# Moving an output projection into the block of the attention loop, with its first units among the last attention steps

## The reference

```
x  : (8, 1024, 256)
xn = layernorm(x)
q, k, v = xn Wq' + bq, xn Wk' + bk, xn Wv' + bv      16 heads of 64
out = softmax(q k' / 8) v                              per batch and head
attn = out Wo' + bo                                    Wo: 256 x 1024
moe  = routed experts (64, top 8, at most 128 tokens each) + shared expert
y = x + attn(xn) + moe(xn)
```

## Time and profile before

| | |
|---|---|
| runs | 3563.14, 3563.44, 3565.11 us |
| profiled execution: its own time | 3562.05 us |
| its span, first to last instruction | 3560.3 us |
| mean granted TensorE clock | 0.992 of 2.4 GHz |
| PE busy | 3494.3 us, 98% |
| POOL, DVE, ACT busy | 2708.6, 2494.6, 1679.5 us |

### The profile page before, as it was taken

How to read it: one execution, slowest core, us unless ns; L and a number is a source line. 1 busy time by engine, 2 the same in 40 slices (tenths; PEclk the granted TensorE clock), 3 DMA queues, 4 the chain that set the end, 5 groups by cost and what they waited for, 6 DMA issues and landing times. The chain is left out here.

```text
span 3560.3 us, 60153 instructions
## 1 busy us (share of the span) xinstructions
PE 3494.3 (98%) x16416; PEld 2101.2 (59%) x16416; DVE 2494.6 (70%) x3255; ACT 1679.5 (47%) x3122; POOL 2708.6 (76%) x2339
## 2 busy tenths in 40 slices
PE   7999799999999999999999999999999999999899
PEld 6888555555555555555555555555555555555487
DVE  7888577777777777777777777777777777777344
ACT  4555344444444444444444444444444444444343
POOL 2111288888888888888888889888888888889521
PEclk9999899999999999999999999999999999999899
DMA  8777856666666666666666666666666666664396
GB/s 248 234 223 223 222 129 153 165 166 170 171 166 169 169 168 169 167 170 172 175 175 175 175 175 172 168 168 167 166 170 169 169 168 169 167 167 119 124 322 226
DMA packets 393678, 635.57 MB, mean 179 GB/s; under 512 B 48097, under 2 KB 214689, under 8 KB 393633
## 3 DMA queue, kind: packets, MB, share of 16 engines
q1 hardware_dynamic: 370848, 603.54, 61.2%
q0 software_dynamic: 14336, 23.08, 3.1%
q10 hardware_dynamic: 8448, 8.39, 0.7%
HBM read 306.91 MB, written 126.12 MB: 122 GB/s over the span
## 5 line engine op out<-in xcount | busy, mean ns | idle before, releaser
L1132 DVE TENSOR_REDUCE merged<-psum 128x1 f32<-128x1024 f32 x1024 | 1206.1, 1220 | 725.7 <-PE psum L857 724.9
L1093 ACT ACTIVATE probs<-psum 128x512 f32<-128x512 f32 x2048 | 1083.4, 600 | 1157.8 <-PE psum L831 826.6
L1314 POOL TENSOR_TENSOR sums<-sums,probs 128x512 f32<-128x512 f32 x768 | 980.0, 1276 | 96.5 <-ACT probs L1093 40.9
L1315 POOL TENSOR_TENSOR sums<-sums,probs 128x512 f32<-128x512 f32 x768 | 981.4, 1278 | 0.0
L872 PE MATMUL psum<-probs,v_sb 128*64 128x512 f32 x4096 | 931.9, 597 | 0.0
L828 PE MATMUL psum<-q_full,k_full 128*128 128x512 f32 x2048 | 877.1, 428 | 0.9 <-DVE low L1142 0.9
L831 PE MATMUL psum<-q_rest,k_rest 65*128 65x512 f32 x2048 | 811.9, 396 | 1.8 <-DMA q_rest<-minus_max 1.8
L872 PEld LDWEIGHTS psum<-probs,v_sb 128*64 128x64 f32 x4096 | 284.2, 137 | 561.0 <-issue 498.3
L828 PEld LDWEIGHTS psum<-q_full,k_full 128*128 128x128 f32 x2048 | 387.9, 189 | 197.1 <-issue 94.3
L1164 DVE RECIPROCAL sum_all<-sum_all 128x128 f32<-128x128 f32 x512 | 448.9, 919 | 28.3 <-ACT sum_all L1101 28.3
L831 PEld LDWEIGHTS psum<-q_rest,k_rest 65*128 65x128 f32 x2048 | 389.6, 190 | 63.5 <-DMA q_rest<-minus_max 2.1
(11 more groups left out here) (153 smaller groups left out, 3049.1 us busy)
## 6 DMA issues: line engine op xcount, KB each, us to landing
x_t<-xt SPq DMA_DIRECT2D x118, 1024.0 KB
k_full<-high SPq DMA_DIRECT2D x256, 256.0 KB
v<-values SPq DMA_DIRECT2D x64, 512.0 KB, 3.4
w_qk<-wqk_parts SPq DMA_DIRECT2D x64, 512.0 KB, 4.1
v_sb<-v SPq DMA_DIRECT2D x64, 512.0 KB, 4.7
q_full<-high SPq DMA_DIRECT2D x128, 256.0 KB
q_full<-low SPq DMA_DIRECT2D x128, 256.0 KB
k_rest<-low SPq DMA_DIRECT2D x128, 256.0 KB
```

Source lines behind the costliest of these rows:

```text
L1093: nc.scalar.activation(probs[:, kt, h, :], ring[ring_place(g, j) % RING], ACT.Exp, scale=SCALE).then_inc(probs_ready, 1)
L1132: nc.vector.tensor_reduce(out=merged[:, col:col + 1], in_=work[:, 2 * h:2 * h + 2, :].rearrange("p b c -> p (b c)"), axis=AX, op=ALU.max, ...
L1314: nc.gpsimd.tensor_tensor(sums[:, half, 0, :], first[:, 0, :], probs[:, kt, 0, :], ALU.add)
L1315: nc.gpsimd.tensor_tensor(sums[:, half, 1, :], first[:, 1, :], probs[:, kt, 1, :], ALU.add).then_inc(sums_added, 1)
```

## The change

The output stage is no block of its own any more; its instruction lists stand behind attention's in the same block. It gets its memory from attention's tiles: Wo's parts lie over `x_t`, `wo32` over `w_qk`, the loaded `ot` (`ot32_0`, `ot32_1`) over `high` and `low`, the high parts over `q_full` and `k_full`, the low parts over `q_rest` and `k_rest`, and x, `moe`, `rest` and y over `probs`. Therefore x and `moe` can only be loaded when attention's last P times V and last additions are done.

Work is put among the last steps:

- SP: `wo32`, `bv`, `bo` are loaded at the start of step 62 (`wo32` was loaded at the start of attention), unit 0's `ot` at the start of step 63, unit 1's after that. Behind the last store of attention come x and `moe` of unit 0, a wait for them, x and `moe` of unit 1, and then the loop over units 2 to 15.
- ACT: the weights' high part in four pieces in groups 2 and 3 of step 62 (`split_weights`), unit 0's high part in eight pieces in groups 1 and 2 of step 63 (`split_piece`), unit 1's at its end.
- DVE: the weights' low part in group 0 of step 63, the low parts of units 0 and 1 at its end, with the constant between.
- PE: at the end of step 63 both products of unit 0 with the constant's 32 small ones between, and then step 64 with the last `add_up` and P times V.

```diff
+    with ExitStack() as over:
+        ot32 = [over.enter_context(nc.sbuf_tensor(f"ot32_{par}", [P, PAIRS, HALF], F32)) for par in range(2)]
     high = sb("high", [P, 2, 2, N], F32R)
     low = sb("low", [P, 2, 2, N], F32R)
...
@@ tensor, end of step @@
+            if is_step(s, NP - 1):
+                pe.wait_ge(quad_reduced, QUADS * NP)
+                pe.wait_ge(wo_high, PIECES)
+                pe.wait_ge(wo_low, 1)
+                project(0, 0, 0)
+                pe.wait_ge(loaded_b, 2 * DMA)
+                for c in range(KD):
+                    for h in range(PAIRS):
+                        last = nc.tensor.matmul(psum[:, 7, c:c + 1], wo32[:, h, c * P:(c + 1) * P], bv[:, h:h + 1],
+                                                start=(h == 0), stop=(h == PAIRS - 1))
+                last.then_inc(const_filled, 1)
+                pe.wait_ge(y_weighted, NP)
+                project(0, 0, 1)
...
+        def output():
+            pe.wait_ge(const_ready, 1)
+            project(1, 1, 0)
+            project(1, 1, 1)
+            turn(0, 0)
+            project(2, 0, 0)
+            project(2, 0, 1)
+            turn(1, 1)
...
@@ scalar, step @@
+                    if is_step(s, NP - 2) and g >= 2 and n % 4 == 3:
+                        split_weights(2 * (g - 2) + n // 4)
+                    if is_step(s, NP - 1) and g >= 1 and n % 2 and 4 * g + n // 2 < 12:
+                        split_piece(4 * g + n // 2 - 4)
...
+            if is_step(s, NP - 1):
+                split_high(1, 1)
@@ vector, step @@
+                if is_step(s, NP - 1) and g == 0:
+                    dve.wait_ge(wo_high, PIECES)
+                    nc.vector.tensor_tensor(wo[:, LOW], wo32[:], f32(wo[:, HIGH]), ALU.subtract).then_inc(wo_low, 1)
+            if is_step(s, NP - 1):
+                split_low(0, 0)
+                dve.wait_ge(const_filled, 1)
+                dve.wait_ge(loaded_b, 2 * DMA)
+                nc.vector.tensor_tensor(const[:], psum[:, 7, 0:KD], bo[:], ALU.add).then_inc(const_ready, 1)
+                split_low(1, 1)
@@ sync, step @@
+            if is_step(s, NP - 2):
+                sp.wait_ge(lows_ready, 4 * NP)
+                sp.dma_start(wo32[:], io["wo"].rearrange("(h p) d -> p h d", p=P)).then_inc(loaded_w, DMA)
+                sp.dma_start(bv[:], io["bv"]).then_inc(loaded_b, DMA)
+                sp.dma_start(bo[:], io["bo"]).then_inc(loaded_b, DMA)
+            if is_step(s, NP - 1):
+                for half in range(2):
+                    sp.wait_ge(out_stored[half], DMA * PAIRS)
+                sp.wait_ge(placed, DMA * SHUFFLES * NP)
+                sp.wait_ge(quad_filled, QUADS * NP)
+                load_output(0, 0, 0)
...
             if att:
                 shift_out(s, par, 1)
+            if is_step(s, NP - 1):
+                for n in range(2):
+                    sp.wait_ge(ot_loaded[n], DMA)
+                load_output(0, 1, 1)
...
+        def output():
+            sp.wait_ge(pv_done, 4 * NP)
+            sp.wait_ge(sums_added, 14 * NP)
+            sp.wait_ge(scattered, DMA * NP)
+            load_rest(0, 0)
+            sp.wait_ge(xm_loaded, 2 * DMA)
+            load_rest(1, 1)
+            for half in range(2):
+                sp.wait_ge(out_stored[half], DMA * NP)
+            with sp.Fori(1, UNITS // 2) as i:
+                for par in range(2):
+                    u = i * 2 + par
+                    alone(sp, (loaded_w, DMA), (ot_loaded[0], DMA * u), (ot_loaded[1], DMA * u),
+                          (xm_loaded, 2 * DMA * u), (ot_low, 2 * (u - 1)), (rest_ready, u - 1))
+                    load_output(i, par, par)
+                    load_rest(u, par)
...
-        sp.dma_start(keep["wo32"][:], io["wo"].rearrange("(h p) d -> p h d", p=P)).then_inc(keep["loaded_w"], DMA)
-        for half in range(2):
-            sp.wait_ge(out_stored[half], DMA * NP)
```

More of the change, by code:

```diff
@@ new lines, in project @@
+        def project(u, par, c):
+            if not known(u, 2):
+                pe.wait_ge(project_copied, KD * (u - 2) + c + 1)
+            n = 0
+            for batch in range(2):
+                for t, o in ((HIGH, HIGH), (LOW, HIGH), (HIGH, LOW)):
+                    if c == 0:
+                        if o == HIGH and t == HIGH:
+                            pe.wait_ge(ot_high, 2 * u + batch + 1)
+                        elif o == LOW:
+                            pe.wait_ge(ot_low, 2 * u + batch + 1)
+                    for h in range(BATCH):
+                        last = nc.tensor.matmul(psum[:, 4 + 2 * par + c, :],
+                                                wo[:, t, batch * BATCH + h, c * P:(c + 1) * P],
+                                                ot(par, o, batch)[:, h, :], start=(n == 0), stop=(n == 3 * PAIRS - 1))
+                        n += 1
+            last.then_inc(project_filled, 1)
@@ new lines, in turn @@
+        def turn(u, par):
+            pe.wait_ge(project_copied, KD * (u + 1))
+            if known(u, 2):
+                pe.wait_ge(probs_ready, SCORES * NP)
+                pe.wait_ge(sum_copied, 2 * NP)
+                pe.wait_ge(out_ready, 2 * NP)
+            else:
+                pe.wait_ge(y_ready, 2 * (u - 1))
+            for n in range(2):
+                for t in range(2):
+                    for c in range(KD):
+                        tok = slice((2 * n + t) * P, (2 * n + t + 1) * P)
+                        last = nc.tensor.transpose(psum[:, 2 * par + n, t * D + c * P:t * D + (c + 1) * P],
+                                                   projected[par][:, c, tok], ident[:])
+                last.then_inc(y_filled, 1)
@@ L1094, in exp, with split_weights, split_piece, split_high @@
                                  ).then_inc(probs_ready, 1)
+        def split_weights(n):
+            if n == 0:
+                act.wait_ge(loaded_w, DMA)
+            pairs = slice(n * PAIRS // PIECES, (n + 1) * PAIRS // PIECES)
+            nc.scalar.copy(wo[:, HIGH, pairs], wo32[:, pairs]).then_inc(wo_high, 1)
+        def split_piece(n):
+            batch, h = divmod(n, BATCH)
+            if h == 0:
+                act.wait_ge(ot_loaded[batch], DMA)
+            last = nc.scalar.copy(ot(0, HIGH, batch)[:, h, :], ot32[0][:, n, :])
+            if h == BATCH - 1:
+                last.then_inc(ot_high, 1)
+        def split_high(u, par):
+            for batch in range(2):
+                act.wait_ge(ot_loaded[batch], DMA * (u + 1))
+                nc.scalar.copy(ot(par, HIGH, batch), ot32[par][:, batch * BATCH:(batch + 1) * BATCH]
+                               ).then_inc(ot_high, 1)
+        def project_out(u, par):
+            for c in range(KD):
+                act.wait_ge(project_filled, KD * u + c + 1)
+                if c == 0 and not known(u, 2):
+                    act.wait_ge(y_filled, 2 * (u - 1))
+                nc.scalar.activation(projected[par][:, c, :], psum[:, 4 + 2 * par + c, :], ACT.Identity,
+                                     bias=const[:, c:c + 1]).then_inc(project_copied, 1)
+        def store(v, par):
+            if not known(v, 1):
+                act.wait_ge(y_stored, DMA * v)
+            act.wait_ge(y_ready, 2 * (v + 1))
+            act.dma_start(out_v[bass.ds(v, 1)].rearrange(parts), y[:, par]).then_inc(y_stored, DMA)
+        def output():
+            def unit(u, par):
+                act.wait_ge(project_filled, KD * (u - 1))
+                split_high(u, par)
+                project_out(u - 1, 1 - par)
+                store(u - 2, par)
+            act.wait_ge(const_ready, 1)
+            project_out(0, 0)
+            unit(2, 0)
+            unit(3, 1)
+            with act.Fori(2, UNITS // 2) as i:
+                unit(i * 2, 0)
+                unit(i * 2 + 1, 1)
+            project_out(UNITS - 1, 1)
+            store(UNITS - 2, 0)
+            store(UNITS - 1, 1)
+            act.wait_ge(y_stored, DMA * UNITS)
         def empty(p, half):
@@ L1270, in _ @@
         run_steps(dve, step)
+        output()
     @block.gpsimd
@@ L1339, in _, with output, unit @@
         head()
+        def output():
+            def unit(u, par):
+                pool.wait_ge(xm_loaded, 2 * DMA * (u + 1))
+                if not known(u, 2):
+                    pool.wait_ge(y_ready, 2 * (u - 1))
+                nc.gpsimd.tensor_tensor(rest[:, par], x_out[:, par], moe_sb[:, par], ALU.add).then_inc(rest_ready, 1)
+            unit(0, 0)
+            unit(1, 1)
+            with pool.Fori(1, UNITS // 2) as i:
+                unit(i * 2, 0)
+                unit(i * 2 + 1, 1)
         run_steps(pool, step)
         pool.wait_ge(scattered, DMA * NP)
+        output()
     @block.sync
```

293 lines of the change are left out of this document (92 added, 201 removed).

## The result

The changed kernel takes 3573.65 us (median of 10, 3570.12 to 3576.67) where the kernel before, run beside it, takes 3564.18: ratio 1.0026 [1.0018, 1.0034]. It is slower, by about 9 us, and outside my range, which ended at 3569.6. I had forecast 3562.0.

What follows compares the result with a forecast made beforehand. PE was taken to bound the output stage at 12.08 us a unit; filled holes and removed waits give 10.6 us, POOL's block and the clock take 9.2 back, gaining 1.4: forecast 3562.0, range 3553.5 to 3569.6.

Steps and rivals of the forecast that it cites:

- DVE holds up POOL: Step 63: each DVE subtraction costs POOL its full 2.29 us; hidden values at 3332.2, third P times V block 9.2 later.
- Rivals A and B: Step 63: subtractions don't delay hidden values, 3552.9 to 3555.1, chance 0.22 (A); POOL's short instructions precede second subtraction, 3559.1, 0.15 (B).
- Rival D: Step 63: POOL never lets Wo's subtraction in, DVE stands over 2 us; 6.8 us slower or more, 3570 to 3572; chance 0.07.
- PE's fill: After step 63's third block: 24 products 5.6 us, small ones 3.5, 24 slow-clock products 7.3; last `add_up` starts at 3356.7.
- SP's late list: Unit 2's ot loads last, behind x and `moe` of units 0 and 1; PE waits 6.8 us, unit 3 starts at 3394.5.
- Rival C: Output stage's x and `moe` transfers take 8.8 us each from issue to landing; 6.2 us slower, 3569.6; chance 0.11.
- Later units load in 10.9 to 12.08 us and PE takes 12.08, so nothing is late again.: Output stage after unit 3: loads keep up with PE's 12.08 us a unit, so no further loss.
- Sum: Up to unit 3's start: 3395.95 before less 3394.5 predicted, 1.4 us gained; profiled execution 3560.6, median 3562.0.
- the lock: Experiments' theory for the output stage: a store issued with a round's loads stretches it past PE's 12.08 us and stays there.
- ENGINES: Experiments' theory for the output stage's rounds: what engines do at the same time makes the loads slow.

## Why the prediction was wrong

- **DVE holds up POOL: right.** I said hidden values 6.9 us later, a wait of 4.8, the third block 9.2 later. With the execution's own start of step 63 taken off (its first P times V starts at 3291.61, before's at 3287.98, so 3.63 us; 2.95 of them stand there from step 0 on, see below) the block ends 8.85 us later. The wait is 2.84 us instead of 4.8: in the execution's own time the hidden values came 0.9 earlier than I said (3334.94 less 3.63 is 3331.3), and PE was free 1.0 later (3332.24 less 3.63 is 3328.6), behind a P times V block of 5.71. Rivals A and B have no place: the expert's last product (`DN`) starts at 3335.08, and POOL's two short instructions each took a full turn behind a subtraction. Rival D falls too: the subtraction of Wo's part took 2.98, so stood 0.7 us.
- **PE's fill: right in kind, 1.7 us short.** From the third block's end to `add_up` 18.1 us, where my terms give 16.4. The small products took 4.75 instead of 3.5, and the clock fell before they were done: it shows 0.50 from 3352, they end at 3354.06. In before it fell only at their end. The run with the late store did the same fill in 15.0 with 3.63 for the small ones, the clock at 1.00 all the time. The same code; between executions this term moves by 3 us.
- **SP's late list: right.** From x's issue at 3368.10 to that of unit 2's `ot` at 3378.62 it takes 10.5 us (predicted 10.1). PE waits 7.39 (predicted 6.8). Rival C has no place either: 5.1 and 5.4 us for the pairs, not 8.8. Unit 3 starts at 3399.43 instead of 3394.5. Of these 4.9 us, 1.7 are the fill and the other 3 or so the head, the late start of this execution described below.
- **The step that failed: "Later units load in 10.9 to 12.08 us and PE takes 12.08, so nothing is late again."** I took the length of a round from before as if it were the transfer's own, whatever else runs (and even there one round took 12.4, from 3391.00 to 3403.39). In before the stores came 5.6 us or more behind the loads. After the wait of 7 us they come 1.5 to 2.2 us behind them, the same bytes take 12.9 us, and the twelve rounds that follow take 155.5 us (3389.77 to 3545.31) where PE's pace makes 145.0: 10.6 us too much, of which 174.2 - 164.35 = 9.8 show from unit 3's start on, since PE had a little data in hand. Runs show it from three sides: the store later takes it out of the changed kernel (10.7 us between the medians), one late load puts it into before, and the store later takes it out there too. What keeps the store there is not PE but the lists of ACT and DVE, as the run with `ot` early shows. The rule I had needed is not that the loads fit into PE's time, but that they fit with the store at its worst place.
- **Sum.** Without the lock, unit 3's start 3.5 us later than before's would be the whole loss, 3 us of it from that head; with the late store unit 3 starts at 3392.68 and the profiled execution takes 3558.99, where I had worked out 3394.5 and 3560.6.

The head is a spread between executions that I had not counted. The first P times V of step 0, in code that no kernel here changes, starts at 438.43 in before and at 441.38 in after:

```profile
441.38 3.65 PE L923 MATMUL psum<-probs,v_sb 128*64 128x512 f32 x16
```

In runs with the head of before it stands at 439.13 (unit 2 late) and 444.48 (store later). So it belongs to the execution, and a comparison of two profiles, one each, carries up to 6 us of it.

What the early store costs can be put together in part. The first two rounds of before, with no store in them, took 10.6 and 10.7 us, the changed kernel's first one 11.2 (one of before's, the third, took 11.9, and no run says why); with the early store it is 12.9, with the late one 11.1. At the 380 GB/s or so that most slices show, 0.52 MB would be 1.4 us (an estimate). So the early store costs its bytes and 0.3 to 0.9 us more, and the late one less than its bytes, since it moves at the round's end. What stays open is that remainder: the view shows dips while both run, and no run tells what makes them. ENGINES isn't excluded as a part of it: with the store, the work around it moves too. And why the clock falls at, in or never behind the small products, in executions of the same code, is open.

## What to carry to other kernels

A round in which all loads are waited for has no fixed length: it depends on where in it the stores fall. Where the consumer is only a microsecond or so slower than the round, as here 12.08 against 10.6 to 12.4, one late transfer can move the stores to the front of the loads. They stay there if the lists make the store wait for work on the newest load, as here the rounding and the subtraction. Look for the time from load issue to store issue and for what stands ahead of the store, and put it where the loads are nearly done. And a subtraction of 2.3 us on one engine is a price for short instructions on the other, each in its turn; it is worth a wait to place it behind them.

## What the runs showed of the hardware

- A round with 3.15 MB of loads and 0.52 MB of a store took 12.9 us (282 GB/s) with the store issued 1.6 us behind the loads, and 11.1 (330 GB/s) with it 8 us behind, where its bytes moved after nearly all of the loads'. Rounds without a store took 10.6 to 11.2, and one 11.9.
- POOL's instructions of 0.46 and 0.45 us took 2.40 and 2.49 beside DVE's subtractions of 2.28 and 2.54: one turn each, not a share.
- Thirty-two products with one column, PE without a hole, took 3.63 us with the clock at 1.00 and 4.75 us where it fell while they ran. It then showed 0.50, the 1.2 GHz level, for 4 us and more, though PE never waited:

```profile
3352.00:3356.00 4.00, 4.00 (x15) 3.61 (x16) 1.90 (x2) 0.00 (x0) 0.00 (x0) 0.50 0.00 0
```
